# Edge frames of a graph network computed in seven spans of 224 columns instead of in 98 batches of 16

## The reference

```
layer 0:  hn[i]  = mean over edges e with dst[e] = i of x[src[e]]
          x      = layernorm(x + hn)
layer 1:  R[e]   = relu(weight[e] * w1 + b1) @ w2 + b2            # 64 hidden, 384 numbers an edge
          Y[e]   = spherical harmonics (l = 0, 1, 2) of edge_attr[e] / |edge_attr[e]|
          m[e]   = sum over paths of R[e] x Y[e] x features(src[e]) x Wigner 3j   # 8 scalars, 8 vectors
          x      = layernorm(x + segment_sum(m, dst))
```

## Time and profile before

| | us |
|---|---|
| median of 3 runs | 5211.26 |
| lowest, highest | 5207.74, 5223.45 |
| the profiled execution | 5212.62 |
| its span in the trace | 5210.5 |

### The profile page before, as it was taken

How to read it: one execution, slowest core, us unless ns; L and a number is a source line. 1 busy time by engine, 2 the same in 40 slices (tenths; PEclk the granted TensorE clock), 3 DMA queues, 4 the chain that set the end, 5 groups by cost and what they waited for, 6 DMA issues and landing times.

```text
span 5210.5 us, 49008 instructions
## 1 busy us (share of the span) xinstructions
PE 2764.2 (53%) x14521; PEld 2488.3 (48%) x14521; DVE 2896.8 (56%) x4976; ACT 747.1 (14%) x1220; POOL 3731.3 (72%) x3539
## 2 busy tenths in 40 slices
PE   0000000000000000013899999999999999999972
PEld 0000000000000000013888888888888888888862
DVE  7333333343333333344677777777777777777764
ACT  1111011011111111100111111111111111111110
POOL 6766666666666666666788787787778778777855
PEclk9999999999999999999999999999999999999985
DMA  3111111111111111111112222222221222222211
GB/s 77 28 24 27 24 27 27 25 29 25 25 27 26 27 27 24 25 26 27 36 43 43 43 43 43 43 43 43 41 43 43 43 43 43 43 43 43 43 28 20
DMA packets 178117, 182.73 MB, mean 35 GB/s; under 512 B 62498, under 2 KB 146101, under 8 KB 171575
## 3 DMA queue, kind: packets, MB, share of 16 engines
q1 hardware_dynamic: 71478, 127.76, 8.7%
q0 software_dynamic: 106624, 54.80, 7.7%
HBM read 119.70 MB, written 62.61 MB: 35 GB/s over the span
## 4 chain that ended last, share of the span: by engine, by line
PE 22%; POOL 15%; issue 8%; DVE 7%; another core or an unknown queue 0%; DVEq 0%; DMA 0%; ACT 0%; POOLq 0%; ACTq 0%
PE ps_m L709 14%; POOL got L511 13%; PE ps_r L724 5%; PE ps_r L726 3%; DVE halves L1150 2%; DVE prod L1188 2%; POOL back L494 1%; POOL terms L498 1%; DVE prod L1196 1%; DVE part L1170 1%; PE ps_m L693 1%; POOL ngot L482 0%; DVE pick L1082 0%; DVE prod L1105 0%
## 5 line engine op out<-in xcount | busy, mean ns | idle before, releaser
L511 POOL DMA_INDIRECT got<-x_d,idx x1568 | 1849.0, 1179 | 530.5 <-issue 499.6
L457 POOL DMA_INDIRECT got<-in_x_dram,idx x1536 | 1453.5, 946 | 740.5 <-issue 483.5
L709 PE MATMUL ps_m<-halves,ident 128*128 128x128 f32 x6272 | 1534.0, 412 | 70.7 <-DVE halves L1150 49.5
L709 PEld LDWEIGHTS ps_m<-halves,ident 128*128 128x128 f32 x6272 | 1270.5, 209 | 215.5 <-DVE halves L1150 65.4
L672 PE MATMUL ps_r<-hot_j,hot_p 128*128 128x98 bf16 x1568 | 145.8, 282 | 2058.2 <-DVE hot_j L803 933.9
L672 PEld LDWEIGHTS ps_r<-hot_j,hot_p 128*128 128x128 bf16 x1568 | 124.9, 141 | 2079.2 <-DVE hot_j L803 908.8
L724 PE MATMUL ps_r<-wc,hid 128*128 128x256 f32 x3136 | 952.6, 386 | 28.4 <-DVE prod L1196 14.0
L726 PEld LDWEIGHTS ps_r<-wc,hid 128*128 128x128 f32 x3136 | 599.6, 191 | 84.6
L726 PE MATMUL ps_r<-wc,hid 128*128 128x128 f32 x3136 | 605.5, 275 | 0.1
L1188 DVE TENSOR_TENSOR prod<-ps_r,f_along 128x1024 f32<-128x1024 f32 x392 | 476.3, 1215 | 148.8 <-PE ps_r L726 52.5
L724 PEld LDWEIGHTS ps_r<-wc,hid 128*128 128x128 f32 x3136 | 525.1, 198 | 47.1 <-issue 14.6
(11 more groups left out here) (138 smaller groups left out, 1658.3 us busy)
## 6 DMA issues: line engine op xcount, KB each, us to landing
run_d<-runs_t SPq DMA_DIRECT2D x196, 256.0 KB
hid<-weight_t SPq DMA_DIRECT2D x98, 512.0 KB
got<-x_d,idx POOLq DMA_INDIRECT x1568
got<-in_x_dram,idx POOLq DMA_INDIRECT x1536
frame_d<-frame SPq DMA_DIRECT2D x98, 72.0 KB
frame<-frame_d SPq DMA_DIRECT2D x98, 72.0 KB
ngot<-run_d,pos_c POOLq DMA_INDIRECT x196
unit<-in_edge_attr_dram SPq DMA_DIRECT2D x1, 2058.0 KB
```

The lines of the kernel that those rows point to most:

```text
L457: pool.indirect_dma_start(got[k][:, t, :], None, x, bass.IndirectOffsetOnAxis(ap=(idx_start if first else idx)[k][:, t:t + 1], axis=0)).th ...
L511: pool.indirect_dma_start(got[k][:, t, :], None, x1_d, bass.IndirectOffsetOnAxis(ap=idx[k][:, t:t + 1], axis=0)).then_inc(got2_landed[k], 16)
L709: mm = pe.matmul(ps_m[:, k, g * SG * D:(g + 1) * SG * D], ident[:, :], halves[g % 2][:, :, :, v].rearrange("p t o -> p (t o)"), start=(v = ...
```

## The change

Frames are no longer made batch by batch. The 1568 columns are cut into seven spans of 224 columns (14 batches, 7 pairs). At the head of a span DVE makes all frames of the span in one block of instructions with 224 columns instead of 16, then runs the 14 batches of the span without frame work. The first span's block comes after the first pair of batches. One frame buffer of 224 x 9 floats for each partition and its five helpers lie in the room of x1_sb, which is not used before the node chunks. SP stores a span's frames with one DMA ahead of the run stores of that span. The block works on the unit vectors in place, which saves the copy uvec; the block's waits are for constants. The marks of a loop round on DVE fall from 40 to 4. DVE's and SP's one loop becomes seven.

```
+SPANS = 7
+SPAN = COLS // SPANS
+SPAN_PAIRS = PAIRS // SPANS
-STEPS = {"layer0": 40, "chunks": 18, "layer1": 14}
+STEPS = {"layer0": 4, "chunks": 18, "layer1": 14}
...
-        uvec = sb("uvec", [P, T, 3])
-        small = sb("small", [P, 6, T])
+        span_room = x1_sb[:, :, :].rearrange("p j f -> p (j f)")
+        frame_s = span_room[:, 0:SPAN * 9].rearrange("p (t c a) -> p t c a", c=3, a=3)
+        small = span_room[:, SPAN * 9:SPAN * 14].rearrange("p (c t) -> p c t", t=SPAN)
...
# SP
+            def store_frames(n):
+                sp.wait_ge(frame_ready, n + 1)
+                sp.dma_start(frame_rows[:, n * SPAN * 9:(n + 1) * SPAN * 9],
+                             frame_s.rearrange("p t c a -> p (t c a)")).then_inc(frame_stored, 16)
             def layer0(i):
                 for k in range(2):
                     b = 2 * i + k
-                    sp.wait_ge(frame_ready, b + 1)
-                    sp.dma_start(frame_rows[:, bass.ds(b * (T * 9), T * 9)],
-                                 frame[k][:, :, :, :].rearrange("p t c a -> p (t c a)")
-                                 ).then_inc(frame_stored[k], 16)
                     sp.wait_ge(runs_turned, b + 1)
...
-            with sp.Fori(0, PAIRS) as i:
-                layer0(i)
+            for n in range(SPANS):
+                store_frames(n)
+                with sp.Fori(n * SPAN_PAIRS, (n + 1) * SPAN_PAIRS) as i:
+                    layer0(i)
...
-                        sp.wait_ge(frame_stored[k], 16 * PAIRS)
+                        sp.wait_ge(frame_stored, 16 * SPANS)
# DVE
-            def make_frame(b, k):
-                cut = unit[:, bass.ds(b * T, T), :]
-                s.mark(dve.tensor_scalar(uvec[:, :, :], cut, 0.0, None, ALU.add))
-                s.settle()
-                n0, n1, n2 = (uvec[:, :, c] for c in (1, 2, 0))
-                f = frame[k]
+            def make_frames(n):
+                if n > 0:
+                    dve.wait_ge(frame_stored, 16 * n)
+                cut = unit[:, n * SPAN:(n + 1) * SPAN, :]
+                n0, n1, n2 = (cut[:, :, c] for c in (1, 2, 0))
+                f = frame_s
... (the same arithmetic, 18 instructions, now 224 columns each)
-                dve.tensor_copy(f[:, :, 2, 0], n2).then_inc(frame_ready, 1)
+                s.mark(dve.tensor_copy(f[:, :, 2, 0], n2))
+                s.settle()
+                dve.sem_inc(frame_ready, 1)
...
                     make_hot(b, k).then_inc(hot_ready, 1)
-                    if not first:
-                        dve.wait_ge(frame_stored[k], 16 * i)
-                    make_frame(b, k)
...
-            loop(layer0, PAIRS)
+            layer0(0, True)
+            make_frames(0)
+            for n in range(SPANS):
+                if n > 0:
+                    make_frames(n)
+                start, first_pair, per = s.base + s.n, max(n * SPAN_PAIRS, 1), STEPS["layer0"]
+                with dve.Fori(first_pair, (n + 1) * SPAN_PAIRS) as i:
+                    s.base, s.n = start + (i - first_pair) * per, 0
+                    layer0(i, False)
+                    assert s.n == per, s.n
+                s.base, s.n = start + ((n + 1) * SPAN_PAIRS - first_pair) * per, 0
```

More of the change, by code:

```diff
@@ L218, in build_program @@
         frame_ready = sem("frame_ready")
-        frame_stored = pair("frame_stored")
+        frame_stored = sem("frame_stored")
         got1_landed = pair("got1_landed")
@@ L955, in _ @@
             s.settle()
-            def make_frame(b, k):
-                cut = unit[:, bass.ds(b * T, T), :]
-                s.mark(dve.tensor_scalar(uvec[:, :, :], cut, 0.0, None, ALU.add))
-                s.settle()
-                n0, n1, n2 = (uvec[:, :, c] for c in (1, 2, 0))
-                f = frame[k]
-                sign, inv, n0i, n1i, sn0, q = (small[:, c, :] for c in range(6))
+            def make_frames(n):
[4 more added lines that the diff above has]
+                f = frame_s
+                sign, inv, n0i, n1i, sn0 = (small[:, c, :] for c in range(5))
                 s.mark(dve.tensor_scalar(sign, n2, 0.0, 2.0, ALU.is_ge, ALU.mult))
@@ L976, in make_frame @@
                 s.settle()
-                s.mark(dve.tensor_tensor(q, sn0, n0i, ALU.mult))
+                s.mark(dve.tensor_tensor(inv, sn0, n0i, ALU.mult))
                 s.mark(dve.tensor_tensor(f[:, :, 0, 2], n1, n0i, ALU.mult))
@@ L981, in make_frame @@
                 s.mark(dve.scalar_tensor_tensor(f[:, :, 1, 1], f[:, :, 0, 2], -1.0, sign, ALU.mult, ALU.mult))
-                s.mark(dve.tensor_scalar(f[:, :, 0, 1], q, -1.0, 1.0, ALU.mult, ALU.add))
+                s.mark(dve.tensor_scalar(f[:, :, 0, 1], inv, -1.0, 1.0, ALU.mult, ALU.add))
                 s.mark(dve.tensor_tensor(f[:, :, 1, 2], sign, f[:, :, 1, 2], ALU.subtract))
@@ L987, in make_frame @@
                 s.mark(dve.tensor_scalar(f[:, :, 2, 2], n1, -1.0, None, ALU.mult))
-                s.mark(dve.tensor_copy(f[:, :, 0:2, 0], uvec[:, :, 1:3]))
-                dve.tensor_copy(f[:, :, 2, 0], n2).then_inc(frame_ready, 1)
+                s.mark(dve.tensor_copy(f[:, :, 0:2, 0], cut[:, :, 1:3]))
+                s.mark(dve.tensor_copy(f[:, :, 2, 0], n2))
+                s.settle()
+                dve.sem_inc(frame_ready, 1)
             def scan(b, k):
```

## The result

| | before | after |
|---|---|---|
| median of 7 runs, us | 5214.71 | 5233.79 |
| lowest, highest | 5207.74, 5223.45 | 5216.95, 5241.78 |
| the profiled execution | 5212.62 | 5231.91 |
| end of layer 0's edge loop | 2255.6 | 2277.7 |

The ratio is 1.0037, 95% interval 1.0025 to 1.0049: slower by 0.4%. The forecast was 4981. All of the loss lies in the edge loop (+22.1 us between the two profiles); what follows it takes 3 us less than before.

What follows compares the result with a forecast made beforehand. POOL's gathers, 20.0 us a batch, were taken to bound layer 0's loop except where DVE is late. From 5212.6, -246 + 6 + 3 + 7 gave 4983, 4981 against the median; range 4953 to 5065 for 8 in 10.

Steps and rivals of the forecast that it cites:

- Step 1: Layer 0's edge loop: without 19 frame instructions and increments a batch on DVE, POOL's pauses go, -246 us.
- both kinds of batch: DVE's batches in layer 0 without frames: quick 5.4 us, drawn-out at most 12.5 us, both under POOL's 20.0.
- rival C: Wait for hot_counted before hot_p: increments stay late, one stall in five batches, 190 us more, 5173; chance 0.06.
- odd gaps: POOL's issue waits in layer 0: a gather some 2 us late now and then, 28 us, expected to stay.
- Step 2: Span heads on DVE: seven frame blocks of 18 instructions, 8.2 us each, hidden; between 0 and 24 us, taken 6.
- Step 3: First frame block, after batches 0 and 1: batch 4's gathers between 0 and 13 us late, taken 3.
- Step 4: POOL's gathers beside DVE's wide frame blocks are slowed: between 0 and 57 us, taken 7.
- Steps 5 and 6: SP's seven larger frame stores cost nothing; PE and ACT have no instruction changed and idle most of the stage.
- rival A: Frame blocks: the port rule in full, gathers lose the blocks' whole length, 57 us instead of 7, 5033; chance 0.06.
- B: Span heads exposed: POOL waits out every frame block in drawn-out form, 154 us more, some 5137; chance 0.05.
- D: Before hot_p: a 20 us stall in every batch with nothing to clear it, 5457; chance 0.04.

Runs made afterwards that it cites:

- a_nocount: The changed kernel, but PE counts only the last batch's edges and DVE waits for no count before hot_p: 5156.88 us.
- a_half: The changed kernel, but PE does 8 of the 16 matmuls of each batch, still one increment a batch: 5182.73 us.
- group 1: Follow-up runs on one chip, leaving out or altering PE's counting in the kernels after and before; the kernel before took 5227.71 us there.
- a_inc16: The changed kernel, but each of PE's 16 matmuls a batch increments hot_counted, same computation: 5236.83 us.
- n_bare: The changed kernel without PE's counts and one-hot operands in all but the first two batches: 4909.01, 4926.64 and 4891.61 us in three groups.

## Why the prediction was wrong

**Step 1 failed: -246 us taken, +22 us measured.** It has two parts, and each failed for its own reason.

It said that POOL's pauses would go because "both kinds of batch fit under 20 us". DVE's own steps did as it said: 19 fewer increments, and the step waits are gone. But it counted DVE's increments alone. The increment behind PE's 16 matmuls and 16 weight loads a batch is late too, up to 79.9 us, the more so the more of them PE runs, and rival C named the place: the wait for hot_counted. C had one stall in five batches, with 10 us of each lost; there were 37 in 96 batches, 25 us each, and POOL lost 265 us to them. The step took from the earlier trace rows that this wait was worth 79.3 us, as a fixed size. But the increments were as late before the change:
```profile
505.07 1.49 PE L672 MATMUL ps_r<-hot_j,hot_p 128*128 128x98 bf16 x16 [17.63 <-issue]
586.46 2.29 DVE L801 TENSOR_TENSOR hot_p<-ps_r,dst_p 128x2048 bf16<-128x2048 f32 x1 [26.07 <-remote]
```
The longest of the waits in the earlier trace rows, 26.07 us, ended 586.46 - 506.56 = 79.9 us after its matmuls, with an increment recorded 0.13 us before; the four other long ones ended 44 to 56 us after theirs. The wait was short and rare most likely because DVE, held up by its own late steps, came to it late; no run separates this. This row could have warned: it is the lateness of the increment that had to be priced, not what was left of it as a wait.

And it took 16 x 1.25 = 20.0 us for POOL's pace with all waits removed. On a chip of this kind that is the pace between pauses. Without any pause (a_nocount, a_half) it is 22.40. Before, a batch took 22.82, so 0.42 x 96 = 40 us was all that POOL left to gain at the pace from batch 28 on, and 67 us with the faster start. Had the count never been late, the loop would have ended near 2189, as that of a_nocount in group 1 did, and the kernel at about 5146; the forecast by this sum would have been -67, not -246. No row of the kernel before shows this limit. The 28 us of odd gaps, a gather that "comes some 2 us late now and then whoever waits", are no sign of it: on the faster chip, where the limit is absent, they are 490.0 - 1536 x 0.304 = 23 us, one gap of 2 us in seven batches.

From the two, the sum: -67 for the pauses as far as POOL allows, +89 for the stalls before hot_p (2277.7 - 2188.8), together +22; and so the loss. The two terms set loops of different measurements side by side; within group 1 the stalls are worth 2263.8 - 2188.8 = 75 us (a_inc16 against a_nocount).

**Step 2, right in the sum, partly by luck.** The block was to take 8.2 us. Its timeline runs from 661.97 to 669.74 + 0.34 = 670.08, 8.1 us, with the reciprocal at 1.55 (said 1.56) and the copy of 448 at 0.51 (said at most 0.70). Two-operand instructions on strided rows took 0.44 to 0.56 us, above my 0.39, and one-operand ones 0.28 to 0.58. The 18 durations add up to 9.1 us, not 8.2; the block is shorter because neighbours that do not wait for each other overlap. It was hidden: on the faster chip it left 3.1 us of waits in seven blocks. On the first chip DVE waited another 29.20 us behind it anyway.

**Step 3, right.** The gathers of batch 4 were to be due near 106 us. The row at 106.51 has 0.30 us of idle time before it, as have its neighbours; the 6.39 us before batch 4 are gone.

**Step 4, right.** Gathers average 950 ns after against 946 before, 5.7 us in sum where 7 were taken, and 948 in both on the faster chip: nothing of the bound of 57. Beside a block single gathers are longer, 1.02, 1.11 and 1.16 us in the block at 595 us on the faster chip and one of 1.81 us in the block at 662 us above, so a block costs 0.5 to 1.2 us and not its 8.1. The one long gather, 5.25 us beside the 5.06 us tensor_tensor, stands in the kernel after as well. The Trainium skill's rule ("SBUF — State Buffer", section "SBUF: two separate sides") did not price the blocks; rival A falls.

**Steps 5 and 6.** SP cost nothing. That no instruction of PE changes was true, and it misled: PE's part in the loop changed most.

**Rivals.** B did not happen, the pauses are not at heads of spans alone. D had 20 us before every hot_p; the mean was 939.4 / 98 = 9.6 us, and pauses of POOL did clear it every eighth batch. C was right in mechanism and place, and 61 us too cheap (5234 - 5173): stalls were nearly twice as many and cost POOL more. Its chance of 0.06, and 0.04 for slower, was too little: C's place was already the third of the waits that I had listed. The measured 5234 lies between C's 5173 and D's 5457, where no rival stood.

**Open.** What delays the increments of PE, and before the change those of DVE, on the chip measured; what makes a pair of gathers long once a batch there; and whether these are one thing. For one thing speaks that PE's increments in a_inc16 come mostly in multiples of 0.70 us (550 of the 644 distances over 0.5 us between 300 and 2200 us), and that 1.400 us a gather is twice that; no run tests it. That the 22.40 us belong to the gathers alone rests on two kernels with different PE work agreeing to 0.01 us, and in a_half DVE goes on 0.13 us behind PE's increment in most batches; n_bare never ran on such a chip. Whether pacing POOL would cure the lateness where it exists was tried only where it does not.

A rival is untested: the recording of the trace itself. Every execution timed here has a recorded span, so none shows the kernel with nothing recorded. On the chips with late increments the traces hold 23,600 to 25,600 increments of semaphores, on the others 66,000 to 70,000 for nearly the same programs, so records are lost exactly where increments are late. Whether both have one cause, or the recording is it, these runs do not tell. No chip was seen in both conditions, and the first kind was measured only at the beginning, in the first measurement and in group 1; that the chip makes the difference, and nothing else that changed in between, is likely and not shown.

## What to carry to other kernels

Idle time between busy stretches of an engine is a gain only if the engine can hold its pace without it: look for a stretch that has no pause, or make one by leaving out what causes the waits, before multiplying the pace out. When a change removes one kind of late signal, price every other wait that is served in the same way, and do not take its present size, since it may be hidden behind the wait that goes: measure instead how long after the awaited instruction the waiting one starts (79.9 us here, behind a wait of 26). Time a change on more than one chip where its reason is a wait that the instructions themselves do not explain.

## What the runs showed of the hardware

- The same kernel took 5215 and 5228 us (the first measurement and group 1) and 4915 to 4920 us on five other chips, all Trainium2. Between the two profiles of the kernel before lie 292 us; 247.5 of them are in the edge loop, where POOL has its pauses on one chip and none on the other; gathers (946 and 948 ns) are alike. Behind the loop the difference is 44 us, which was not followed up.
- On a chip of the first kind an unbroken row of indirect DMAs of 128 rows ran at 1.25 us each for about the first 15 batches (some 240 DMAs), and then at 1.400 us on average, with a pair of long ones in each batch. On the second kind 1.265 us (20.24 / 16) held to the end.
- On the first kind PE's increment came up to 79.9 us after the matmul while POOL issued gathers, before the change as after it; DVE went on 0.13 us after the increment. On the second kind it came 0.01 us after the matmul. The lateness went with the number of PE's instructions and not of its increments (16 increments instead of one: 23.14 against 23.30 us a batch; half the matmuls: 39.9 us late in most batches). With an increment on each matmul they came 2.1 or 2.8 us apart, and the transfers of the gathers were not behind (DMA share 0.00 from 694 to 699 us).
- Strided float32 rows of 224 columns took 0.44 to 0.56 us with two operands, where the contiguous ones of the node chunks took 0.39.
